# A decoder layer on one core: the layer norms' reciprocal roots, from an integer first guess with three refinements on VectorE to a first guess by ScalarE's Ln and Exp with one

## What is computed

```python
def _layernorm(x, axis=-1, eps=1e-05):
    m = jnp.mean(x, axis=axis, keepdims=True)
    v = jnp.var(x, axis=axis, keepdims=True)
    return (x - m) / jnp.sqrt(v + eps)
...
x = x + _L0_attn_ref(_layernorm(x), norm_w, Wq, Wkv, Wout, Wg)
x = x + _L0_xattn_ref(_layernorm(x), ctx_1024, ctx_1024)
x = x + _L0_ffn_ref(_layernorm(x), Wg, Wup, bup, Wdown, bdown)
```

## Time and profile before

| | |
|---|---|
| Median of 3 runs | 515.9 us (515.74 to 517.25) |
| Profiled execution, its own time | 517.08 us |
| Its span, first to last instruction | 515.3 us |
| Busy: PE / PEld / DVE / ACT / POOL | 456.6 / 372.8 / 389.6 / 329.5 / 253.8 us |
| Mean granted clock of TensorE | 0.972 of full speed |
| Chain that ended last | PE 57%, DVE 19%, ACT 9%, issue 6% |
| Start, until batch 0 is in its regular steps | 0 to 36 us |
| Six steady batches, about 43.5 us each | 68 to 330 us |
| Batch 7 with the rest of batch 6 | 330 to 373 us |
| Rest of batch 7 with tiles 0 to 2 | 373 to 405 us |
| Experts | 405 to 493 us |

### The profile page before, as it was taken

How to read it: one execution, slowest core, us unless ns; L and a number is a source line. 1 busy time by engine, 2 the same in 40 slices (tenths; PEclk the granted TensorE clock), 3 DMA queues, 4 the chain that set the end, 5 groups by cost and what they waited for, 6 DMA issues and landing times.

```text
span 515.3 us, 12330 instructions
## 1 busy us (share of the span) xinstructions
PE 456.6 (89%) x3500; PEld 372.8 (72%) x3500; DVE 389.6 (76%) x1359; ACT 329.5 (64%) x1001; POOL 253.8 (49%) x398
## 2 busy tenths in 40 slices
PE   1679998999999999999999999986798998999980
PEld 1457786877678688687777868764576888999980
DVE  4765567987888788888888878888788746765566
ACT  3558866875776686687757758753543665776650
POOL 4500005167455625636654462585264785666761
PEclk9999999999999999999999999998898998999995
DMA  8990000000000000000000000299301142222239
GB/s 269 368 234 1 1 0 3 1 17 16 10 0 26 10 5 15 21 5 10 21 10 0 26 10 5 68 197 152 74 22 49 41 115 62 69 67 62 64 105 226
DMA packets 43875, 31.66 MB, mean 61 GB/s; under 512 B 3795, under 2 KB 40071, under 8 KB 43840
## 3 DMA queue, kind: packets, MB, share of 16 engines
q1 hardware_dynamic: 39936, 24.22, 19.0%
q0 software_dynamic: 3472, 6.49, 4.0%
q10 hardware_dynamic: 432, 0.53, 0.3%
HBM read 18.91 MB, written 13.04 MB: 62 GB/s over the span
## 4 chain that ended last, share of the span: by engine, by line
PE 57%; DVE 19%; ACT 9%; issue 6%; POOL 4%; SPq 2%; DMA 1%; DVEq 0%; ACTq 0%; POOLq 0%
PE zb L819 8%; PE sc L858 6%; PE ob L887 6%; PE xb L936 5%; PE ob L1098 5%; PE zb L1098 4%; PE xb L961 3%; ACT pT L677 3%; PE tb_a L871 2%; PE tb_a L819 2%; PE tb_b L871 2%; PE sc L819 2%; ACT p_sb L670 2%; PE sc L852 2%; ACT p_sb L668 2%
## 5 line engine op out<-in xcount | busy, mean ns | idle before, releaser
L661 ACT ACTIVATE qk<-zb 128x512 f32<-128x512 f32 x64 | 38.3, 598 | 66.8 <-PE zb L819 66.8
L530 POOL TENSOR_TENSOR spare_p<-tri 128x1 f32<-128x1 f32 x71 | 14.7, 207 | 122.9 <-DVE xn L1295 64.8
L610 POOL DMA_INDIRECT results_by_token<-y_sb,row_i x59 | 59.4, 1006 | 21.0 <-issue 20.8
L668 ACT ACTIVATE p_sb<-sc,nmx 128x128 f32<-128x128 f32 x128 | 47.0, 368 | 33.3 <-DVE nmx L1214 33.0
L670 ACT ACTIVATE p_sb<-sc,nmx 128x256 f32<-128x256 f32 x128 | 61.0, 476 | 0.0
L858 PE MATMUL sc<-qk 64*128 64x256 f32 (+1 forms) x512 | 60.6, 356 | 0.2 <-ACT qk L661 0.2
L887 PE MATMUL ob<-pT,v_sb 128*64 128x256 f32 (+1 forms) x512 | 56.4, 342 | 1.0 <-DVE oT L1232 1.0
L858 PEld LDWEIGHTS sc<-qk 64*128 64x128 f32 x512 | 45.1, 190 | 15.6 <-issue 10.2
L543 POOL DMA_INDIRECT tokens_by_expert<-packed,slot_i x48 | 47.7, 993 | 9.3 <-issue 8.1
L1232 DVE TENSOR_TENSOR oT<-ob,pT 128x256 f32<-128x256 f32 x64 | 26.8, 419 | 25.6 <-PE ob L887 25.6
L887 PEld LDWEIGHTS ob<-pT,v_sb 128*64 128x64 f32 x512 | 31.4, 137 | 19.8 <-issue 8.8
(11 more groups left out here) (301 smaller groups left out, 1345.9 us busy)
## 6 DMA issues: line engine op xcount, KB each, us to landing
tokens_by_expert<-padding SPq DMA_DIRECT2D x12, 390.0 KB, 7.4
xg<-tokens_by_expert SPq DMA_DIRECT2D x24, 130.0 KB, 2.2
wup_all<-in_L_ffn_Wup SPq DMA_DIRECT2D x1, 3072.0 KB, 14.2
wdn_all<-in_L_ffn_Wdown SPq DMA_DIRECT2D x12, 256.0 KB, 6.0
wkv_sb<-in_L_attn_Wkv SPq DMA_DIRECT2D x2, 512.0 KB, 6.4
ctx_b<-in_ctx SPq DMA_DIRECT2D x8, 128.0 KB, 2.1
out<-x_all SPq DMA_DIRECT2D x4, 256.0 KB, 3.6
results_by_token<-y_sb,row_i POOLq DMA_INDIRECT x59
```

What stands on the lines that cost most here:

```text
L610: pool.indirect_dma_start(out=ys, out_offset=bass.IndirectOffsetOnAxis(ap=row_i[:, u, a:a + 1], axis=0), in_=y_sb[:, u, a, :], in_offset=None,
L668: act.activation(p_sb[:, w, h, 0:P], sc[:, k, S:S + P], ACT.Exp, bias=nmx[:, w, 0, n:n + 1], accum_out=total[:, w, 0, h:h + 1])
```

## The change

`rsqrt` goes. In its place ACT computes a first guess of the root, exp(-0.5 * ln(v * 2^-k) - 0.5 * k * ln 2), with k = 20 for the first norm and 40 for the others, and DVE does one refinement (three instructions). Ln and Exp are both in one table set, which ACT now loads by an instruction of its own, ahead of its first DMAs; it holds for all exponentials of the kernel. The variance plus epsilon is now computed inside `centre`, ahead of the subtraction of the mean, so that ACT can work on it early.

```diff
-MAGIC = float(0x5F3759DF)
+ROOTS = "natural_log_exp_and_others"
+GELUS = "gelu_and_others"
+INPUT_SHIFT, RESIDUAL_SHIFT = 20, 40
...
         def _(act):
+            act.preload_act_table_set(ROOTS)
             act.dma_start(wq_sb[:, :], wq).then_inc(ld_wq, 16)
...
+            def first_root(k, a, z):
+                act.wait_ge(v_mean2, k + 1)
+                act.activation(first_log[:, a:z], ms[:, a:z], ACT.Ln, scale=2.0 ** -INPUT_SHIFT).then_inc(a_log1, 1)
+                act.wait_ge(a_log1, k + 1)
+                act.activation(first_guess[:, a:z], first_log[:, a:z], ACT.Exp, scale=-0.5, bias=unshift[:, 0:1]).then_inc(a_guess1, 1)
+            def root(b, k):
+                act.wait_ge(v_var, at(b, 2, k + 1))
+                act.activation(log[:, k, :], (brs, brs3)[k][:, :], ACT.Ln, scale=2.0 ** -RESIDUAL_SHIFT).then_inc(a_log, 1)
+                act.wait_ge(a_log, at(b, 2, k + 1))
+                act.activation(guess[:, k, :], log[:, k, :], ACT.Exp, scale=-0.5, bias=unshift[:, 1:2]).then_inc(a_guess, 1)
...
             def step(cur, prev, nxt, s):
+                if prev is not None and s in (4, 7):
+                    root(prev, (4, 7).index(s))
...
             high_k(FIRST)
+            first_root(0, 0, T)
...
                 step(0, None, 1, s)
+                if s == 1:
+                    first_root(1, T, NT)
...
             def tile(n):
+                if n == 0:
+                    up_high(1)
+                    tokens_high(1)
+                    root(B - 1, 0)
+                    act.preload_act_table_set(GELUS)
+                    gelu(0)
+                    return
...
                 tile(n)
+            act.preload_act_table_set(ROOTS)
+            root(B - 1, 1)
             act.wait_ge(pe_XN, B)
...
             act.activation(el[:, :, :], dl[:, :, :], ACT.Exp).then_inc(a_el, 1)
+            act.preload_act_table_set(GELUS)
...
-            def rsqrt(link, out_, val, n):
-                y, a, t = nwy[:, 0:n], nwa[:, 0:n], nwt[:, 0:n]
-                link(dve.tensor_single_scalar(t.bitcast(I32), val.bitcast(I32), 1, ALU.logical_shift_right))
-                link(dve.tensor_scalar(y.bitcast(I32), t.bitcast(I32), -1.0, MAGIC, ALU.mult, ALU.add))
-                for k in range(3):
-                    link(dve.scalar_tensor_tensor(a, y, -0.5, y, ALU.mult, ALU.mult))
-                    link(dve.scalar_tensor_tensor(t, a, 1.0, val, ALU.mult, ALU.mult))
-                    link(dve.scalar_tensor_tensor(y if k < 2 else out_, t, 1.5, y, ALU.add, ALU.mult))
+            def refine(link, out_, val, y, n):
+                a, t = nwa[:, 0:n], nwt[:, 0:n]
+                link(dve.scalar_tensor_tensor(a, y, -0.5, y, ALU.mult, ALU.mult))
+                link(dve.scalar_tensor_tensor(t, a, 1.0, val, ALU.mult, ALU.mult))
+                link(dve.scalar_tensor_tensor(out_, t, 1.5, y, ALU.add, ALU.mult))
...
             def centre(link, src, dst, variance):
...
                 link(ins)
+                dve.tensor_scalar(variance[:, :], bmv[:, :, 1], LN_EPS, None, ALU.add).then_inc(v_var, 1)
...
-            def deviation(link, dst):
-                link(dve.tensor_scalar(dst[:, :], bmv[:, :, 1], LN_EPS, None, ALU.add))
-                rsqrt(link, dst[:, :], dst[:, :], T)
+            def deviation(b, k, link):
+                dst = (brs, brs3)[k]
+                dve.wait_ge(v_var, at(b, 2, k + 1))
+                dve.wait_ge(a_guess, at(b, 2, k + 1))
+                refine(link, dst[:, :], dst[:, :], guess[:, k, :], T)
```

More of the change, by code:

```diff
@@ L123, in decoder @@
         nwa = sb("nwa", [P, NT])
-        nwy = sb("nwy", [P, NT])
+        first_log = sb("first_log", [P, NT])
+        first_guess = sb("first_guess", [P, NT])
+        unshift = sb("unshift", [P, 2])
+        log = sb("log", [P, 2, T])
+        guess = sb("guess", [P, 2, T])
         xrn = sb("xrn", [P, T, D])
@@ L311, in decoder @@
         a_kv, v_kv = sem("a_kv"), sem("v_kv")
+        v_mean2, a_log1, a_guess1 = sem("v_mean2"), sem("a_log1"), sem("a_guess1")
+        v_var, a_log, a_guess = sem("v_var"), sem("a_log"), sem("a_guess")
         p_kv, p_q, p_sum, p_ret, p_pack, p_keep, p_cell, p_chain = (
@@ L1138, in _ @@
         def _(dve):
+            for k, shift in enumerate((INPUT_SHIFT, RESIDUAL_SHIFT)):
+                dve.memset(unshift[:, k:k + 1], -0.5 * shift * float(np.log(2.0)))
             dve.memset(ones[:, :], 1.0).then_inc(consts_v, 1)
@@ L1173, in first_moments, with first_scale @@
                 return ins
-            def first_scale(a, z):
-                link1(dve.tensor_scalar(ms[:, a:z], mv[:, a:z, 1], 1.0 + RMS_EPS, LN_EPS * RMS_EPS, ALU.mult, ALU.add))
-                rsqrt(link1, rs1[:, a:z], ms[:, a:z], z - a)
+            def first_scale(k, a, z):
+                dve.tensor_scalar(ms[:, a:z], mv[:, a:z, 1], 1.0 + RMS_EPS, LN_EPS * RMS_EPS, ALU.mult, ALU.add).then_inc(v_mean2, 1)
+                dve.wait_ge(v_mean2, k + 1)
+                dve.wait_ge(a_guess1, k + 1)
+                refine(link1, rs1[:, a:z], ms[:, a:z], first_guess[:, a:z], z - a)
             dve.wait_ge(ld_x, 16)
@@ L1182, in _ @@
             link1(first_moments(0, T))
-            first_scale(0, T)
-            CHAIN = 50
+            first_scale(0, 0, T)
+            CHAIN = 32
             sent = [0]
@@ L1237, in v_out, with centre @@
                 dve.tensor_copy(v_sb[:, t, half * 8:half * 8 + 8, 0:DH], src[:, :].rearrange("p (h d) -> p h d", h=8)).then_inc(v_V, 1)
-            def centre(link, src, dst):
+            def centre(link, src, dst, variance):
                 for t in range(T):
@@ L1261, in first_residual @@
                 dve.wait_ge(v_x1, at(b, 1, 1))
-                centre(link, x1b, xn2).then_inc(v_xn2, 1)
+                centre(link, x1b, xn2, brs).then_inc(v_xn2, 1)
             def kv_low(b, t):
@@ L1290, in second_residual @@
                 dve.wait_ge(v_x2, at(b, 1, 1))
-                centre(link, x2b, xc3).then_inc(v_xc3, 1)
+                centre(link, x2b, xc3, brs3).then_inc(v_xc3, 1)
             def scale_third():
@@ L1370, in step @@
                     if s == 7:
-                        deviation(link, brs3)
+                        deviation(prev, 1, link)
                         route_a(prev, link)
@@ L1383, in step @@
                     if s == 4:
-                        deviation(link, brs)
+                        deviation(prev, 0, link)
                 if older is not None and s == 0:
@@ L1425, in _ @@
             link1(first_moments(T, NT))
-            first_scale(T, NT)
+            first_scale(1, T, NT)
             batch(0, None, 1, chain())
@@ L1602, in _ @@
             tokens(1)
-            deviation(link, brs)
+            deviation(b, 0, link)
             read_state(b, 0, 0)
@@ L1616, in _ @@
             tokens(3)
-            deviation(link, brs3)
+            deviation(b, 1, link)
             route_a(b, link)
```

## The result

The changed kernel takes 508.4 us (median of 4 runs, 507.5 to 508.9) against 516.6 us (4 runs, 515.7 to 518.0) of the kernel before on the same chip: a ratio of 0.984, 95% interval 0.981 to 0.986. The forecast was 507.0, with 503.5 to 510.8. The gain is under 2% and clear of no change. The profiled execution took 508.93 us.

The account below looks back on a forecast made before the run. PE was taken to bound steady batches, busy 42.05 of 43.50 us. Loop 6.6, batch 7 2.0, start 1.1 and 0.1, end -0.9 sum to 8.9 us off the 515.9 us median: 507.0 us, range 503.5 to 510.8.

Parts of the forecast that it names:

- The loop's size: Six steady batches: PE's waits for `rg` and `prod` behind the step-4 root go, 1.1 us a batch, 6.6 us in all.
- Batch 7, the rest of batch 6: Written-out part, mostly bounded by DVE: shorter roots in steps 4 and 7 together win 2.0 us.
- The 1.2 us for the root of step 4: Batch 7, step 4: the shorter root removes a PE wait like the loop's and gives 1.2 us.
- at most 0.2 us on a path with slack: Steady batch: variance moved into `centre`, ahead of the subtraction POOL waits on, costs at most 0.2 us, covered by slack.
- The 0.8 us for the root of step 7: Batch 7, step 7: shorter root leads to an attention output on which PE waits 0.96 us; wins 0.8 us (0.3 to 1.0).
- The start: Before the loop: the first norm's 14 roots win 1.1 us, the two roots of batch 0 win 0.1 us.
- The delay of 1.28 us: Start: the table load ahead of ACT's first DMA delays that DMA by 1.28 us; bounded from -0.8 to +0.5.
- The end: End of batch 7: three moved table loads, with Ln and Exp, delay gelu and `xn3T`; sum -0.9 us (-2.5 to +1).
- (1): Steady batches: only part of the step-4 wait goes, 0.6 us instead of 1.1 a batch; 510.0 us, chance 0.17.
- (2): End: a table switch holds ACT longer than its load, two on the path adding 2.6 us; 509.6 us, chance 0.05.
- (3): Loop: slower, since ACT waits in order for the variance and delays PE's scores; 516.6 to 519.6 us, chance 0.02.
- (4): Loop: nothing moves, PE's waits return under another name, start's gain is given back at the end; 515.7 us, chance 0.06.

Follow-up runs that it names:

- step4_alone: Changed kernel, but the third norm's root (step 7 and its like at the end) computed the old way on VectorE; batches 42.17 us, ratio 0.979.
- var_in_step4: Changed kernel, but in batch 7 alone the variance for the step-4 root is computed first in step 4, not in step 3; batch 7 42.53 us, ratio 0.984.
- combined: Changed kernel with batch 7's variance moved to step 4, PE filled with repeated transposes, and the last batch's roots done the old way; batch 7 41.36 us, ratio 0.983.
- old_end: Changed kernel, but the last batch's two roots computed the old way on VectorE, with table loads moved off the path; 507.7 us, ratio 0.982.
- two_more_loads: Changed kernel plus one more Gelu and root table load ahead of the third norm's root at the end; logits 2.57 us later, ratio 0.987.
- before_root_in_idle: Kernel before, with its long root moved from the end of step 4 into step 5, where VectorE waits for PE; batches 43.33 us, ratio 1.001.
- three_refinements: Changed kernel with three refinements instead of one at the step-4 root; batches 42.95 us, ratio 0.989.
- pe_filled: Changed kernel, but in batch 7 PE repeats transposes ahead of its waits for `rg` in steps 4 and 6; batch 7 43.61 us, ratio 0.978.

## Why the prediction was right, and where it was wrong

**Right in sign, range and place.** The loop gives nearly everything, through the root in step 4 alone; VectorE's time in step 7 is worth nothing there (`step4_alone`).

**The loop's size.** Forecast 1.1 us a batch, measured 1.31. I had added the idle times 0.76 and 0.29 and some hundredths for each restart. From start to start behind the projection the transpose came 0.91 us earlier and the state half 1.33 (17.36 and 18.47 us now, 18.27 and 19.80 before). The idle time in front of a matmul leaves out about 0.15 us each time PE stands still: in an unbroken row the next transpose starts 0.11 us behind the start of one that lasts 0.27 (211.39 and 211.50 in the changed kernel), while idle time counts only from that one's end. "Some hundredths" was too little. The bounds held.

**The step that failed is "Batch 7, the rest of batch 6", with its 2.0 us; 0.06 came.** Of its two terms one failed and one came. The 1.2 us for the root of step 4 did not reach the last transposes: these are 0.85 us later and not 1.2 earlier, 2.05 us off. What I had costed as "at most 0.2 us on a path with slack", the variance in `centre`, is the first part of this. In the loop the path has slack. In batch 7 VectorE itself is the bound in step 3 and later (before, 354.00 to 373.02, it is busy for 16.25 us and PE for 11.66), its instructions lie beside POOL's rotation, and 0.35 us became 0.94; PE's wait then doubled and its clock fell. `var_in_step4` gives 0.8 of it back. With PE kept busy as well, in `combined`, the last transposes stand at 36.84 us, 1.1 earlier than before the change; but there the fall inside the wait of 3.85 us is gone too, which the kernel before has, so the other 1.2 us are not all a loss that the change had made. That the root of step 4 is worth about what I said when step 3 is not in its way, the pair with the plan moved shows (1.22, up to step 6).

The 0.8 us for the root of step 7 came, as 0.91. The reason given was right: an attention output on which PE waits 0.96 us, now 0.40. The rows say how. Before, `rg` of step 7 stands behind the root and PE's attention output behind it starts 1.57 us behind the transposes, now 1.21; and `row_i`, behind the root too, holds up the `oT` for which PE waits, so that the next output starts 2.04 us behind that one, now 1.49. The two make 0.36 and 0.55. This is read from one execution of the kernel before against four with the short root; no run changes the step 7 root alone at a clock of 1.00. At half clock, where PE is later anyway, it is worth 0.1 to 0.2. So the total of this step is a loss that I had at nothing, set off by a gain that I had right.

**The start** gave 1.07 for 1.2. The 14 roots gave 1.0 us for 1.1, since VectorE stands still for 0.69 us until the pair is done, and the two roots of batch 0 about 0.1. The load on ACT runs from 0.80 to 2.08 us, but the DMA issues behind it were not held up by it: ACT's queue issues the first at 0.82, as before the change at 0.80. The delay of 1.28 us, which the prediction has as a bound only, did not exist. ACT (ACTq is its DMA queue) in the changed kernel:

```profile
0.80 1.28 ACT L645 ACT_TABLE_LOAD   x1 [0.80 <-PEq L1713]
0.82 0.44 ACTq L646 DMA_DIRECT2D wq_sb<-in_L_attn_Wq  x1
```

**The end** cost 1.0 for 0.9: the two loads and their pair did what the text said (1.20 at `down(0)` for 1.05, 1.49 at the logits for 1.25, 0.80 at `down(3)` for 0.9), and `old_end` takes it all back.

**Rivals.** (1) needed ACT's pair in step 7 to cost PE time, and a stretch beside POOL to fall on `rg` or the maxima; the pair costs nothing, and the stretch fell on the chain (0.72 us). (2) is refuted by `two_more_loads`. (3): ACT never waits for the variance in the loop. (4) is refuted by the batches. The sum was 8.9 and 8.1 came; the loop's 1.4 more and batch 7's 1.9 less make most of the difference, start and end 0.1 less each, and the level of the runs, 516.6 instead of 515.9 before, the other 0.6 us of the median.

**Open:** why the clock falls in batch 7 in one execution and not in another with the same wait; what the step 7 root gives by itself at a clock of 1.00; and what of the 0.94 us is POOL's share was not separated from the instruction's own length.

## What to carry to other kernels

A chain of tiny dependent instructions delays what is behind it in the list, and that costs time beyond the slack of the engine that waits: find that engine's wait first, and only then shorten the chain. Cost an added instruction separately in each written-out stage, since 0.2 us on a path with slack can be 0.9 where that engine is the bound and shares its time with another. Compare two stretches only at the same granted clock: at half clock TensorE hid what the shorter chain of step 7 gives.

## What the runs showed of the hardware

- TensorE's clock in steps 3 to 5 of batch 7 went from 2.4 to 1.2 GHz behind waits of PE of 1.82 us (`var_in_step4`), 1.89 and 2.37 (the plan moved), 2.58 to 2.61 (six executions), and 1.35 followed by 0.73 (`before_root_in_idle`). It did not behind 1.34 followed by 0.74 (before) and not behind 2.61 in `three_refinements`, so the wait's length does not decide alone. Where PE repeated transposes through the waits (`pe_filled`, `combined`) it stayed at 2.4.
- Inside the wait of 3.85 us in step 6 (4.51 in one run), or up to 0.8 us behind it, the clock fell in every kernel but those two. A fall in the last part of batch 7 costs 1.5 us.
- Small VectorE instructions beside POOL's: 2 columns took 0.16 us alone, and 0.35 to 0.80 us beside its rotations and sums; a product of 256 columns took 0.97 instead of 0.42; one of 2 columns ran 1.70 us (L1287 at 352.56), until POOL's product of 1.95 us was over.
- A table load took 1.28 us, with 0.01 to 0.02 us to the ACTIVATE on either side, and held back no DMA issue of the same engine (0.82, 1.29 and 1.82 us with the load, 0.80, 1.26 and 1.74 without).
- Two of the three chips needed some 14 us more behind 400 us, in every kernel, with ACT or PE standing still for stretches of up to 8.6 us; the cause was not looked for.
